# Later attentions of a three-attention kernel: two key blocks folded into 129 columns, one transpose per head, values shifted by a row through DMA

## What is computed

```python
def local_attention(q, k, v):
    ...
    bk, bv = (look_around(bk), look_around(bv))
    ...
    sim = jnp.einsum('bhwid,bhwjd->bhwij', bq, bk)
    i = bt[:, :, None]
    j = btk[:, None, :]
    mask = (i < j) | (i > j + WINDOW) | (j == -1)
    sim = jnp.where(mask, -jnp.finfo(sim.dtype).max, sim)
    attn = jax.nn.softmax(sim, axis=-1)
    out = jnp.einsum('bhwij,bhwjd->bhwid', attn, bv)
```

## Time and profile before

| | |
|---|---|
| median of 3 runs | 1857.42 us (1856.61 to 1857.83) |
| the profiled execution's own time | 1858.28 us |
| its span, first to last instruction | 1856.5 us |
| TensorE / VectorE busy | 1790.4 us (96%) / 1516.9 us (82%) |
| ScalarE / GpSimd busy | 1199.2 us (65%) / 1075.1 us (58%) |
| mean granted TensorE clock | 0.994 |
| bytes moved by DMA, share of 16 engines | 113.53 MB, 19.5% |
| first and last scores of the later attentions (the MLP of layer 0 lies between) | 632.5 us, 1636.5 us |

### The profile page before, as it was taken

One profiled execution on the slowest core, in us unless ns is written; L12 is line 12 of the kernel. 1 busy time (PEld: TensorE's weight loads), 2 busy tenths in 40 slices (PEclk: granted clock), 3 DMA queues, 4 the chain that ended last, 5 costly groups with the idle time before them and its releaser, 6 DMA issues.

```text
span 1856.5 us, 43215 instructions
## 1 busy us (share of the span) xinstructions
PE 1790.4 (96%) x15168; PEld 1527.0 (82%) x15168; DVE 1516.9 (82%) x3861; ACT 1199.2 (65%) x3086; POOL 1075.1 (58%) x1032
## 2 busy tenths in 40 slices
PE   6999999999999999999999999999999999999997
PEld 4777777777999788888888888887888888878886
DVE  6878888875887889889888677788988988966776
...
DMA packets 139667, 116.01 MB, mean 62 GB/s; under 512 B 10440, under 2 KB 138704, under 8 KB 138704
## 3 DMA queue, kind: packets, MB, share of 16 engines
q1 hardware_dynamic: 139472, 113.53, 19.5%
...
...
## 4 chain that ended last, share of the span: by engine, by line
PE 74%; DVE 16%; issue 5%; ACT 5%; POOL 1%; DMA 0%; SPq 0%; DVEq 0%; ACTq 0%; POOLq 0%
PE psum L545 16%; PE psum L547 15%; PE psum L546 15%; PE psum L867 6%; PE psum L835 5%; PE psum L848 5%; PE psum L809 3%; DVE psum L1164 2%; PE psum L646 2%; ACT a_probs L1659 2%; PE psum L881 2%; DVE a_neg_max L1166 1%; DVE q_t L1150 1%; PE psum L660 1%; DVE masked L1292 1%
## 5 line engine op out<-in xcount | busy, mean ns | idle before, releaser
L1761 ACT ACTIVATE b_probs<-masked,neg_max 128x256 f32<-128x256 f32 (+1 forms) x512 | 251.3, 494 | 122.3 <-DVE neg_max L1292 122.3
L1292 DVE CUSTOM_DVE_ANT_0 masked<-psum,mask 128x256 f32<-128x256 f32 (+1 forms) x512 | 177.3, 413 | 74.9 <-PE psum L835 74.9
L545 PE MATMUL psum<-wa_hi,b_h_hi 128*128 128x512 f32 (+1 forms) x576 | 234.7, 407 | 2.2 <-DVE b_h_lo L1232 2.0
L547 PE MATMUL psum<-wa_hi,b_h_lo 128*128 128x512 f32 (+1 forms) x576 | 214.0, 372 | 0.0
L546 PE MATMUL psum<-wa_lo,b_h_hi 128*128 128x512 f32 (+1 forms) x576 | 213.6, 371 | 0.0
L545 PE MATMUL psum<-g_h_hi,wm_hi 128*128 128x512 f32 (+1 forms) x480 | 191.4, 399 | 9.0 <-DVE g_new L1490 4.8
L1973 POOL TENSOR_TENSOR g_in<-g_in,minus_half 128x16 f32<-128x16 f32 x64 | 188.0, 2938 | 4.5 <-DVE g_in L1244 4.5
L547 PE MATMUL psum<-g_h_hi,wm_lo 128*128 128x512 f32 (+1 forms) x480 | 189.7, 395 | 0.0
L546 PE MATMUL psum<-g_h_lo,wm_hi 128*128 128x512 f32 (+1 forms) x480 | 189.6, 395 | 0.0
L1855 ACT ACTIVATE gate<-psum,vec_b 128x512 f32<-128x512 f32 x96 | 66.1, 689 | 157.3 <-PE psum L547 157.1
L545 PE MATMUL psum<-wm_hi,u_hi 128*128 128x256 f32 x576 | 164.3, 285 | 0.1
...
## 6 DMA issues: line engine op xcount, KB each, us to landing
...
```

The costliest lines, as they stand in the source:

```text
L545: nc.tensor.matmul(out, a_hi, b_hi, start=first, stop=False)
L547: return nc.tensor.matmul(out, a_lo, b_hi, start=False, stop=last)
L1292: ins = nc.vector.tensor_tensor_reduce(out[:, at], src[:, at], (mask if now else mask0)[:, at], -1.0, BIG, ALU.add, ALU.min, neg_max[:, r, ...
L1761: ins = nc.scalar.activation(out, src, ACT.Exp, bias=neg_max[:, r, k:k + 1], scale=-1.0, accum_out=row_sum[:, n % 2, 4 * r + k:4 * r + k + 1])
```

## The change

The scores of a query against the block in front and against its own block never both count in one column: key c + 1 of its own block counts from query c + 1 on, key c of the block in front up to query c. So after the scores `maxima` copies the valid scores of the block in front over the masked ones of the block itself (`copy_predicated`, PSUM to PSUM, shifted by one column), and 129 columns per head are left: column 0 is key 0 of the block in front, which the copy has no room for. The tables of q are negated, so the extreme is a minimum, reduced in one instruction for four heads. ScalarE takes the exponentials of 129 columns straight from PSUM. One transpose per head gives 128 of them, now in one bank; ScalarE copies a round in one instruction (`bp_now`), and GpSimd (`select`) parts it into own block (`bp_now`) and block in front (`bp_before`) by two `affine_select`s.

Since the folded columns of the block in front stand one key later, its values are needed turned by one row: SyncE copies `v_tok` to `v_roll`, 127 rows in one DMA and the last row in another (`roll_values`). Column 0 of the probabilities goes by DMA to the DRAM tensor `x_extra`, a float at a time, and comes back transposed as row 0 of `bp_before` in two DMAs (`save_extra`, `place_extra`). When a chunk's keys lie in the third slot they are repeated in slot 0, so that two blocks always lie side by side (`repeat_keys`, two DMAs on every third chunk). `v_tok` has three buffers and `v_roll` two.

`o_low` moves from GpSimd to VectorE, `widen_inverse` from GpSimd to ScalarE, and the orders within a step change on ScalarE, VectorE, GpSimd and SyncE; TensorE's order in a step stays. The core of the diff:

```diff
-    return {NCH - 4: 1, NCH - 3: 6, NCH - 1: 5}.get(n, 4)
+    return {NCH - 4: 1, NCH - 3: 2, NCH - 1: 4}.get(n, 5)
...
+            def roll_values(n):
+                sp.wait_ge(S["v_copied"], g0 + n + 1)
+                if n >= 2:
+                    sp.wait_ge(S["pv_done"], 2 * (g0 + n - 1) + 2)
+                src, dst = v_tok[n % 3], v_roll[n % 2]
+                sp.dma_start(dst[1:P, :], src[0:P - 1, :]).then_inc(S[f"roll{n % 3}"], 16)
+                sp.dma_start(dst[0:1, :], src[P - 1:P, :]).then_inc(S[f"roll{n % 3}"], 16)
+
+            def save_extra(n):
+                sp.wait_ge(S["exp_ready"], 2 * (g0 + n) + 2)
+                sp.dma_start(x_extra[g0 + n].rearrange("k q -> q k"), b_probs[:, :, :, 0].rearrange("p r k -> p (r k)"),
+                             allow_slow_non_contiguous=True).then_inc(S["extra_saved"], 16)
+
+            def place_extra(n, r):
+                sp.wait_ge(S["select_ready"], 2 * (g0 + n) + r + 1)
+                sp.wait_ge(S["extra_saved"], 16 * b_extras(layer, n))
+                sp.dma_start(bp_before[0:1, r, :, :].rearrange("o k q -> o (k q)"),
+                             x_extra[g0 + n, 4 * r:4 * r + 4, :].rearrange("k q -> (k q)").unsqueeze(0)).then_inc(S[f"extra{r}"], 16)
+
+            def repeat_keys(n):
+                sp.wait_ge(S["kt_copied"], g0 + n + 1)
+                for t in (k_t_hi, k_t_lo):
+                    sp.dma_start(t[:, :, 0, :].bitcast(F32), t[:, :, b_slot(n), :].bitcast(F32)).then_inc(S["kt_twice"], 16)
...
             for s in range(-1, B_LAST):
+                if b_chunk(s + 5):
+                    sp.wait_ge(S["rope_ready"], g0 + s + 2)
+                    load(s + 5)
+                if 0 <= s < NCH - 1:
+                    roll_values(s)
+                if b_chunk(s) and not b_batch_first(s):
+                    save_extra(s)
+                    place_extra(s, 0)
                 if s == NCH - 2:
                     sp_mlp(sp, MLP_B, MB, layer, opening=True)
+                if b_chunk(s) and not b_batch_first(s):
+                    place_extra(s, 1)
+                if b_chunk(s + 1) and b_twice(s + 1):
+                    repeat_keys(s + 1)
                 if b_chunk(s - 2):
                     store(s - 2)
                 if b_chunk(s):
                     load_residual(s)
-                if b_chunk(s + 5):
-                    sp.wait_ge(S["rope_ready"], g0 + s + 2)
-                    load(s + 5)
...
-                    for half in (now,) if b_batch_first(n) else (0, 1):
-                        at = (k % 2) * 256 + half * P
-                        mm = nc.tensor.transpose(bank[4 + 2 * r + k // 2][:, at:at + P], b_probs[:, r, k, half, :], ident[:])
+                    mm = nc.tensor.transpose(bank[4 + 2 * r][:, k * P:k * P + P], b_probs[:, r, k, 1:1 + P], ident[:])
                 mm.then_inc(S["pt_ready"], 1)
...
-                pe.wait_ge(S["pt_act"], i + 1)
-                pe.wait_ge(S["pt_dve"], i + 1)
+                pe.wait_ge(S["select_ready"], i + 1)
                 if r == 0:
                     pe.wait_ge(S["v_copied"], g0 + max(n + 1, 2))
                     if n > 0:
                         pe.wait_ge(S["o_scaled"], g0 + n)
-                now = a_keys(n)[1]
-                blocks = [(n, now)] if b_batch_first(n) else [(n - 1, 1 - now), (n, now)]
+                blocks = [(v_tok[n % 3], bp_now)]
+                if not b_batch_first(n):
+                    blocks.insert(0, (v_roll[(n - 1) % 2], bp_before))
+                    pe.wait_ge(S[f"extra{r}"], 16 * b_extras(layer, n))
+                    pe.wait_ge(S[f"roll{(n - 1) % 3}"], 32 * b_rolls(layer, n - 1))
...
-                for k in range(4):
-                    out = masked[:, r, k, :, :].rearrange("p a q -> p (a q)")
-                    src = bank[4 + 2 * r + k % 2][:, (k // 2) * 256:(k // 2) * 256 + 256]
-                    ins = nc.vector.tensor_tensor_reduce(out[:, at], src[:, at], (mask if now else mask0)[:, at], -1.0, BIG,
-                                                         ALU.add, ALU.min, neg_max[:, r, k:k + 1])
-                ins.then_inc(S["max_ready"], 1)
...
+                    nc.vector.copy_predicated(at[:, :, P + 1:2 * P],
+                                              not_yet[:, 1:P].bitcast(I32).unsqueeze(1).to_broadcast([P, 4, P - 1]),
+                                              at[:, :, 0:P - 1]).then_inc(S["max_ready"], 1)
+                v.wait_ge(S["max_ready"], 2 * i + 1)
+                nc.vector.tensor_reduce(neg_max[:, r, :], at[:, :, P + b_columns(n).start:2 * P], AX.X, ALU.min).then_inc(
+                    S["max_ready"], 1)
...
+            def o_low(n):
+                v.wait_ge(S["o_hi"], g0 + n + 1)
+                if n > 0:
+                    v.wait_ge(S["wo_ready"], g0 + n)
+                nc.vector.tensor_tensor(b_o_lo[:], b_o[:], b_o_hi[:].bitcast(F32), ALU.subtract).then_inc(S["o_lo"], 1)
...
+                if b_chunk(s + 1) and s + 1 > 1:
+                    scale_rotated(s + 1)
                 if b_chunk(s - 1):
                     scale_o(s - 1)
                 if s == NCH - 1:
...
-                if b_chunk(s):
-                    copy_probs(s, 0)
-                if b_chunk(s + 1) and s + 1 > 1:
-                    scale_rotated(s + 1)
...
                 if b_chunk(s + 2) and s + 2 > 1:
                     norms(s + 2, 1)
-                if b_chunk(s):
-                    copy_probs(s, 1)
+                if b_chunk(s - 1):
+                    o_low(s - 1)
+                if b_chunk(s + 3) and s + 3 > 3:
+                    h_low(s + 3)
...
-                if b_chunk(s + 3) and s + 3 > 3:
-                    h_low(s + 3)
                 if b_chunk(s + 1):
                     k_t_low(s + 1)
                     q_t_low(s + 1)
...
+                        src = bank[4 + 2 * r + b][:, j * 256 + P + c0:j * 256 + 2 * P]
+                        h = 4 * r + 2 * j + b
+                        ins = nc.scalar.activation(b_probs[:, r, 2 * b + j, 1 + c0:1 + P], src, ACT.Exp,
+                                                   bias=neg_max[:, r, 2 * b + j:2 * b + j + 1], scale=-1.0,
+                                                   accum_out=row_sum[:, n % 2, h:h + 1])
...
-                b_copy_probs(lambda out, src: nc.scalar.activation(out, src, ACT.Copy), n, r, 0).then_inc(S["pt_act"], 1)
+                nc.scalar.activation(bp_now[:, r, :, :].rearrange("p k q -> p (k q)"), bank[4 + 2 * r][:], ACT.Copy).then_inc(
+                    S["pt_copied"], 1)
...
                 if b_chunk(s):
                     exponentials(s, 0)
+                    exponentials(s, 1)
                 if b_chunk(s - 1):
                     copy_spread(s - 1)
-                if b_chunk(s):
-                    exponentials(s, 1)
                 if s == 0:
                     h_high(s + 3)
+                if b_chunk(s):
+                    copy_probs(s, 0)
                 if b_chunk(s + 2) and s + 2 > 1:
                     copy_qk(s + 2, 1)
                     copy_qk(s + 2, 0)
+                if b_chunk(s - 1):
+                    o_high(s - 1)
                 if b_chunk(s):
-                    copy_probs(s, 0)
+                    copy_probs(s, 1)
                 if b_chunk(s + 3) and s + 3 > 3:
                     h_high(s + 3)
-                if b_chunk(s):
-                    copy_probs(s, 1)
                 if b_chunk(s + 1):
                     k_t_high(s + 1)
                     q_t_high(s + 1)
                 if s == -1:
                     h_high(2)
-                if b_chunk(s - 1):
-                    o_high(s - 1)
+                if b_chunk(s):
+                    widen_inverse(s)
...
+                pool.wait_ge(S["pt_copied"], 2 * (g0 + n) + r + 1)
+                now, before = bp_now[:, r, :, :], bp_before[:, r, :, :]
+                if not b_batch_first(n):
+                    nc.gpsimd.affine_select(before, now, [[0, 4], [-1, P]], ALU.is_ge, 0.0, base=-1, channel_multiplier=1)
+                nc.gpsimd.affine_select(now, now, [[0, 4], [1, P]], ALU.is_ge, 0.0, base=0, channel_multiplier=-1).then_inc(
+                    S["select_ready"], 1)
```

175 lines of the change are left out of this document (79 added, 96 removed).

## The result

The changed kernel takes **2369.8 us** (median of 4 runs, 2368.9 to 2374.6) against 1857.3 beside it: ratio 1.2765, 95% interval 1.2743 to 1.2787. Its profiled execution spans 2372.9 us. The direction was as predicted. The size was not: 2162 us was said, 2290 was the upper end.

A forecast was written before the change was run, and what follows sets the result against it. TensorE was taken to bound the kernel before, the values' DMA path the changed one: 56 x (17.8 - 12.57) = 293 us, plus 12 for other chunks, on 1858 gave 2163, against the median 2162 us; range 1985 to 2290.

The forecast's parts named there:

- the closed path: Values' path through DMA: roll, `save_extra`, `place_extra`, `values`, then the next roll; 17.6 us, 17.8 with repeated keys, sets the step.
- `values`: 1.9 us: Last term of the values' path through DMA: TensorE's `values` take 1.9 us, as in the kernel before.
- rival 3: The clock falls as TensorE stands still: steps of 20.4 us, 2307 us; chance 0.07, shared with another long wait.
- Roll and save: First terms of the DMA path: the 127-row roll lands in 12.9 us, `save_extra` 0.7 us (0 to 3) after it.
- A slow save: Another long wait: an `x_extra` store of single floats taking several us; chance 0.07, shared with rival 3.
- rival 1: The roll spreads over the engines, its path hides, the end-of-step delay decides: 2003 us (1985 to 2030); chance 0.18.
- One engine for 127 rows: The roll: 127 is prime, so one DMA engine moves all rows, 11.0 us of packets; chance about as summed 0.71.
- The end of the step: `o_high` waits for `out_project`, later copies queue: from `out_project`'s end E, scores start at E + 4.5; 3.15 us more, contained in DMA path.
- ScalarE's copies late, 0.3 us: First-round copy stands ahead of q and k copies, `transpose_rotated` waits: 0.3 us of the 0.87 us gain lost.
- VectorE and GpSimd: VectorE has some 0.7 us less work, no cover needed; GpSimd 0.7 us more, has room, costs nothing.
- Bound of the kernel before: TensorE, busy 96%, bounds the 12.57 us step; eight fewer transposes, 0.87 us a step, alone give 52 us less.
- rival 2: Delayed copies don't hold TensorE; with a spread roll 1824 us at best; chance 0.03.

The follow-up runs named there:

- roll126: The changed kernel with the roll's 127 rows split into a DMA of 126 rows and one of a single row: 2216.8 us.
- both: The changed kernel with the roll's 127 rows as 126 + 1 and `o_high` and `o_low` in their old places: 2250.2 us.
- sparse_only: The changed kernel with only the save's 1024 floats stored 512 bytes apart in DRAM: 2513.8 us.
- order: The changed kernel with only `o_high` back at the end of ScalarE's step and `o_low` at the start of VectorE's: 2378.8 us.
- noextra126: The changed kernel with column 0 left out (no save, no places) and the roll as 126 + 1 + 1 rows: 2100.5 us.
- noextra_both: As noextra126, with `o_high` and `o_low` also in their old places: 1906.5 us.
- tcol2: Changed kernel, column 0 through TensorE, roll 126 + 1 + 1, `o_high` in its old place, `o_low` behind the maxima, GpSimd's partings before `rotate_k`: 1871.8 us.
- tcol4: As tcol2, with GpSimd's partings and tables behind VectorE's scaling of q and k: 1884.8 us.

## Why the prediction was right or wrong

- **The steps that failed** are two terms of the closed path; the path itself is right. Medians over the trace: from the roll's issue to the places' 15.1 us, from there to the values 2.3, the values 3.4, together 20.8. The sum had 12.9 + 0.7 = 13.6, then 2.1 and 1.9, together 17.6. So two terms are 1.5 us short each.
- **"`values`: 1.9 us"** is the time at the full clock. TensorE stands still before them (3.97 us in the step shown) and then runs them wholly or in part at the lower level: 3.4 us. The clock had no term in the sum and no part in the range. It was rival 3, with "it takes that waits and work fall badly every time" against it; in most steps they do fall so. The rival's own size, 20.4 us a step, is close to the 20.8 measured, but that is in part luck: it counted slow work in the rest of the step, where there is room for it, and the loss is in the values, where there is none.
- **Roll and save, "12.9" and "`save_extra` ...: 0.7 us (0 to 3)"**: 15.1. The save, which is issued 5 us after the roll, takes 10.0 us from its issue to its landing, and 10.9 from its issue to the places' where the roll is out of the way (roll126, both). But it runs beside the roll, so that little of this shows: with a save that lands fast (sparse_only) the two still take 14.4. By this 0.8 of the missing 1.5 us is the roll, whose rows went for some 12 us (about 1041 to 1053) where 11.0 was taken, and 0.7 the late landing. A slow save stood among the rivals, within a chance of 0.07 and with no time of its own, though no row of before showed a scattered write to DRAM. It makes rival 1's time wrong too: a spread roll gives 2217 us (roll126) and not 2003.
- **From the step to the time**: 56 x (20.8 - 17.8) = 168 of the 208 us that were missing. The rest is at the edges, for which the sum had 12 us in all: from the last scores of layer 0 to the first of layer 1 it takes 244.9 us in place of 226.3, and the first and last steps are long too.
- **One engine for 127 rows**: right, at 26 GB/s for most of it.
- **The end of the step**: right to a tenth. `project_v` waits 2.0 us (109.9 in 56 times), scores at E + 4.48. It is contained in the DMA path (order), as said. Alone it costs 194 us (noextra126 to noextra_both); 3.15 us in each of 54 steps were 170. The clock, which the sum left out, has a part in it (mean 0.934 against 0.991); how large wasn't separated from VectorE's new delays in noextra_both.
- **TensorE at some 80% of the span**: 81%, but this is luck. Both the busy time (by 129 us of slow clock) and the span came out longer than was reckoned.
- **ScalarE's copies late, 0.3 us**: `transpose_rotated` waits for `q_sq` in the changed kernel, 14.3 us in 57 times, at most 0.3. Right.
- **VectorE and GpSimd, "cover: none needed" and "nothing"**: wrong. Their hold on each other adds 1.8 us a step to VectorE in noextra_both against before (1.29 for 0.42, 0.69 for 0.42, 0.88 for 0.69, twice 0.95 for 0.70). It is hidden in the changed kernel by the long path.
- **Bound of the kernel before**: TensorE was named and "the others have just finished when it arrives" was read, but not drawn out. VectorE's loop is 12.49 us, so 0.87 us less on TensorE alone is no gain of 52 us; VectorE has to get shorter by as much. The change does take work off it, and GpSimd's hold puts it back: in tcol2 the two sums of L1318 take 1.83 us together and in tcol4 1.30, so that tcol2's 12.4 us would be some 11.9 without this hold (an estimate from these rows). No run has it so, and none gets below 1871.8 us. The 1824 us of rival 2 is not reached, and whether it can be stays open; the forecast didn't rest on it.
